# Row block 0 in two mapped halves, and early columns for both layers right behind rows 0 and 1

## The chip, the cores and the metric

The kernel runs on one core of a Trainium2 chip, as one program. The metric is device time in microseconds (us) of one execution. All data is float32.

## The reference

The network is two graph layers over N = 8192 nodes with F = 64 features and one dense 8192 x 8192 matrix `adj`:

```
x_drop  = x * (u >= 0.1) / 0.9
x1      = layernorm(x + adj @ x_drop)              # first layer
proj    = tanh(|x1|) * x1 / (|x1| + 1e-8)          # |.| is the row's norm, clipped to 10
support = adj @ proj                               # second layer: adj a second time
out     = arctanh(min(|s|, 0.999)) * s / (|s| + 1e-8) @ kernel + bias     # s: rows of support
result  = layernorm(x1 + out)
```

`adj` is 256 MB, far more than the chip's on-chip memory. The second layer needs `proj`, and row block r of `proj` needs all of row block r of `adj @ x_drop`.

## The kernel before

`adj` is cut into 16 x 16 blocks of 512 x 512 elements (1 MB each), block (r, c) for row block r and column block c. A block is loaded by one DMA from the SP queue into a slot of `ring` (17 slots; at the end two more in `feats`). TensorE multiplies it, transposed, in 4 tiles of 128 contraction rows: `feats[:, 0]` (the dropped x, 64 wide) or `feats[:, 1]` (the projection) is the weight, the block's 512 columns are the moving operand, and sums go to a PSUM bank as 64 x 512. Two matmuls of one step go to the two halves of a bank (partitions 0 to 63 and 64 to 127). One layer of one block is 4 matmuls, both layers are 8. The trace shows each matmul as two records, so a layer of a block is 8 records.

`work_order` writes all steps in one list, and every engine follows it:

- `first`: a block used for layer 1 alone, into `sums_first`, 4 matmuls; it is loaded again later. `hold`: the same, but it stays in the ring until its column is mapped.
- `both`: block (r, c) with c < r, both layers, 8 matmuls into `sums_both`: the column is already mapped when row r comes.
- `early`: block (r, 0) for r = 2 to 15, both layers, right behind the start of row 1, in runs of 5 (`EARLY_RUN`). Bank: `sums_both[0]` for even rows, `sums_part[3]` for odd rows. ScalarE saves the layer 2 half in `support` (L416); VectorE turns the layer 1 half in 8 transposes and adds it to x (`early_end`, L501 to 505).
- `part`: layer 2 alone, for held blocks of a column just mapped or for blocks loaded again, one row or two rows in a bank (`two_halves`, `two_rows`); VectorE adds the bank to `support`.
- `turn`: row block r is complete in layer 1. ScalarE copies one half of the sums (L422), VectorE joins, turns, normalises and maps it (`layer1_join`, `layer1_end`), with a power on GpSimd (L374) and the tanh on ScalarE (L427) between. The semaphore `mapped` then lets TensorE use column r for layer 2.
- `finish`: the final part for one or two rows: the product with the weight matrix, arctanh, the residual and the last layernorm.

Behind each turn the next row's lead (`lead_of`, 7 units of 4 matmuls) needs nothing from it, so that TensorE has work while the turn runs. `HELD` says how many blocks of a row are held, `REREAD` how many blocks are loaded again ahead of a row. `place_blocks` gives each load its slot and the number of releases (`block_released`) that SP waits for.

Row block 0 is 12 `first` and 4 `hold` steps; the 8 chunks of x and u (`xu`, 512 KB each) are loaded between its blocks, one chunk per two column blocks. There are 335 block loads in all.

## Time and profile before

| | |
|---|---|
| median of 3 runs | 938.77 us (938.63 to 939.33) |
| the profiled execution, its own time | 938.78 us |
| span of the profile | 936.5 us |
| between the two | 2.28 us |
| TensorE busy | 898.3 us (96%) |
| DMA | 358.35 MB, 383 GB/s over the span |
| VectorE, ScalarE, GpSimd busy | 287.1, 52.0, 57.4 us |

The span runs from the first to the last instruction. A busy TensorE is one with a matmul record open. The kernel's time outside the span is the same small piece at the launch. The rows themselves stand in a section further down.

### The profile page before, as it was taken

How to read it: one execution, taken by the hardware profiler on the slowest of the kernel's cores; microseconds unless marked ns; L12 is line 12 of the kernel's file. 1: busy time of each engine (PE TensorE's matmuls, PEld its weight loads, DVE VectorE, ACT ScalarE, POOL GpSimd, SP SyncE). 2: the span in 40 equal slices, each digit the busy share in tenths (PEclk: the TensorE clock that was granted, in tenths of full speed). 3: DMA queues.
4: the chain of work that ended last, by engine and by line, in shares of the span. 5: the costliest groups of instructions: out<-in, count | busy, mean ns of one | idle time of the engine just before them, and what ended most of it. 6: DMA issues, size and time to landing. Idle time of an engine off the chain costs nothing.

```text
span 936.5 us, 10555 instructions
## 1 busy us (share of the span) xinstructions
PE 898.3 (96%) x4224; PEld 300.9 (32%) x4224; DVE 287.1 (31%) x1056; ACT 52.0 (6%) x136; POOL 57.4 (6%) x50
## 2 busy tenths in 40 slices
PE   5669999999999999999999999999999999999995
PEld 1113333333333333333333333333333333333332
DVE  1135464322313040403131140402204021056656
ACT  0001010000000000000000000000000000002332
POOL 0000000000000000000000000000000000002322
PEclk9999999999999999999999999999999999999998
DMA  9999999999999999997979989799998999999994
GB/s 378 418 422 421 421 421 416 421 422 420 421 421 421 421 413 421 347 423 270 408 289 400 384 333 375 271 424 385 356 356 304 423 362 354 317 399 421 420 421 182
DMA packets 52319, 358.35 MB, mean 383 GB/s; under 512 B 6320, under 2 KB 8368, under 8 KB 9392
## 3 DMA queue, kind: packets, MB, share of 16 engines
q1 hardware_dynamic: 51696, 357.55, 94.6%
q8 instruction: 34, 0.56, 0.2%
q10 hardware_dynamic: 576, 0.13, 0.1%
q14 instruction: 13, 0.11, 0.0%
HBM read 355.57 MB, written 2.10 MB: 382 GB/s over the span
## 4 chain that ended last, share of the span: by engine, by line
PE 88%; DMA 8%; SPq 2%; DVE 1%; issue 0%; POOL 0%; ACT 0%; DVEq 0%
PE sums_both L698 39%; PE sums_first L652 20%; PE sums_part L661 20%; DMA ring<-adj_dram 8%; PE sums_part L652 4%; PE sums_part L680 3%; PE sums_both L680 3%; SPq L339 1%; PE sums_first L742 0%; PE sums_both L742 0%; SPq L335 0%; DVE rows_in L604 0%; DVE stats L478 0%; DVE mv L481 0%; PE sums_both L737 0%
## 5 line engine op out<-in xcount | busy, mean ns | idle before, releaser
L698 PE MATMUL sums_both<-ring,feats 128*64 128x512 f32 x1696 | 370.1, 592 | 0.5 <-DMA ring<-adj_dram 0.5
L652 PE MATMUL sums_first<-ring,feats 128*64 128x512 f32 x1088 | 247.1, 600 | 26.7 <-DMA ring<-adj_dram 26.7
L698 PEld LDWEIGHTS sums_both<-ring,feats 128*64 128x64 f32 x1696 | 121.7, 137 | 243.0 <-issue 240.9
L661 PE MATMUL sums_part<-ring,feats 128*64 128x512 f32 x816 | 182.9, 593 | 0.0
L652 PEld LDWEIGHTS sums_first<-ring,feats 128*64 128x64 f32 x1088 | 76.7, 138 | 190.6 <-issue 142.1
L488 DVE TENSOR_TENSOR row_saved<-sums_both,row_saved 64x512 f32<-64x512 f32 x15 | 10.2, 682 | 350.9 <-ACT row_saved L422 350.9
L661 PEld LDWEIGHTS sums_part<-ring,feats 128*64 128x64 f32 x816 | 59.2, 137 | 114.2 <-issue 113.6
L374 POOL TENSOR_TENSOR rooted<-base,power 128x8 f32<-128x8 f32 x16 | 27.8, 1737 | 799.8 <-DVE base L514 799.8
L553 DVE TENSOR_TENSOR rows_in<-sums_part,rows_in 128x512 f32<-128x512 f32 x36 | 24.9, 692 | 133.8 <-PE sums_part L661 133.6
L652 PE MATMUL sums_part<-ring,feats 128*64 128x512 f32 x240 | 54.7, 593 | 0.0
L422 ACT COPY row_saved<-sums_first 64x512 f32<-64x512 f32 x16 | 9.3, 580 | 606.0 <-PE sums_first L652 606.0
L498 DVE STREAM_TRANSPOSE turned<-row_saved 32x128 f32<-32x128 f32 x128 | 38.6, 302 | 2.1
L652 PEld LDWEIGHTS sums_part<-ring,feats 128*64 128x64 f32 x240 | 17.0, 137 | 32.9 <-issue 32.0
L680 PE MATMUL sums_both<-ring,feats 128*64 128x512 f32 x112 | 25.2, 592 | 0.0
L680 PE MATMUL sums_part<-ring,feats 128*64 128x512 f32 x112 | 25.2, 592 | 0.0
L498 DVE STREAM_TRANSPOSE turned<-sums_part 32x128 f32<-32x128 f32 x56 | 17.2, 308 | 14.0 <-PE sums_part L680 13.2
L406 ACT ACTIVATE rows_in<-rows_in,shift,rooted 128x64 f32<-128x64 f32 x60 | 20.7, 427 | 6.9 <-POOL shift L367 6.8
L498 DVE STREAM_TRANSPOSE turned<-sums_both 32x128 f32<-32x128 f32 x56 | 17.2, 308 | 10.2 <-PE sums_both L680 9.5
L559 DVE TENSOR_TENSOR rows_in<-sums_part,rows_in 64x512 f32<-64x512 f32 x16 | 10.9, 682 | 27.0 <-PE sums_part L652 26.9
L383 POOL TENSOR_TENSOR rooted<-base,power 128x8 f32<-128x8 f32 (+1 forms) x9 | 13.5, 1496 | 48.5 <-DVE base L570 48.5
L472 DVE TENSOR_SCALAR rows_in<-rows_in 128x512 f32<-128x512 f32 x8 | 3.4, 427 | 40.4 <-DMA rows_in<-xu_dram 40.4
L364 POOL TENSOR_TENSOR rooted<-base,power 128x8 f32<-128x8 f32 (+1 forms) x9 | 13.5, 1496 | 22.3 <-DVE minus_mean L613 19.3
(72 smaller groups left out, 246.6 us busy)
## 6 DMA issues: line engine op xcount, KB each, us to landing
ring<-adj_dram SPq DMA_DIRECT2D x331, 1024.0 KB, 12.7
rows_in<-xu_dram SPq DMA_DIRECT2D x8, 512.0 KB, 20.1
feats<-adj_dram SPq DMA_DIRECT2D x4, 1024.0 KB, 16.2
out_dram<-rows_in SPq DMA_DIRECT2D x15, 128.0 KB, 6.9
out_dram<-rows_in SPq DMA_DIRECT2D x1, 96.0 KB, 2.0
selw<-selector_dram ACTq DMA_DIRECT2D x1, 32.0 KB, 6.6
selw<-weight_dram ACTq DMA_DIRECT2D x1, 32.0 KB, 10.1
bias_sb<-bias_dram ACTq DMA_DIRECT2D x1, 32.0 KB, 12.3
```

The source lines that it names most:

```text
L364: nc.gpsimd.tensor_tensor(rooted[:, 0, own], base[:, 0, own], power[:, 0, own], ALU.pow).then_inc(deviation_ready, 1)
L374: nc.gpsimd.tensor_tensor(rooted[:, :, 0:TB], base[:, :, 0:TB], power[:, :, 0:TB], ALU.pow).then_inc(root_ready, 1)
L383: nc.gpsimd.tensor_tensor(rooted[:, 1, own], base[:, 1, own], power[:, 1, own], ALU.pow).then_inc(norm_rooted, 1)
L406: last = nc.scalar.activation(x_row(r)[:, t, :], x_row(r)[:, t, :], ACT.Identity, scale=rooted[:, 0, i:i + 1], bias=shift[:, i:i + 1])
L488: done(V.tensor_tensor(row_sum[:], sums_both[r % 2][0:F], half_sum[:], ALU.add))
L498: last = V.transpose(turned[q:q + Q, :, f:f + Q], tiles[f:f + Q, :, q:q + Q])
L553: V.tensor_tensor(total, bank[:], total, ALU.add).then_inc(part_added, 1)
L559: done(V.tensor_tensor(total, bank[0:F], total, ALU.add))
L652: last = nc.tensor.matmul(bank[at:at + F], feats[:, which, c * TB + t, :], block_of(slot)[:, t, :], start=start and t < 2, stop=stop and t ...
L661: last = nc.tensor.matmul(bank[F * g:F * g + F], feats[:, 1, c * TB + t, :], block_of(slot)[:, t, :], start=start and t == 0, stop=stop an ...
L680: last = nc.tensor.matmul(early_banks[r % 2][layer * F:layer * F + F], feats[:, layer, t, :], block_of(slot)[:, t, :], start=t == 0, stop= ...
L698: last = nc.tensor.matmul(sums_both[r % 2][layer * F:layer * F + F], feats[:, layer, c * TB + t, :], block_of(slot)[:, t, :], start=begin ...
```

## The change

Row block 0 is loaded in another cut: a 1 MB pack holds two column blocks for 256 of the 512 rows. The kernel runs over all columns for the first 256 rows (8 `top` steps, h = 0), then for the second (h = 1), with matmuls of 256 moving columns; each half has a `turn` of its own, with 2 tiles in place of 4. Directly behind come `begin` and `complete` for (r, 0), r = 2 to 7: `begin` uses tiles 0 and 1 (the first mapped half of column 0) in both layers, `complete` tiles 2 and 3, each 4 matmuls, into six banks. For rows 2 to 5 the block is loaded in two halves of 512 KB (`lower`, `upper`). The lead of row 1 is empty. `early` of column 0 for rows 8 to 12 follows, and behind row 1's turn `early` for (13, 0), (14, 0), (15, 0), later columns 1 of rows 13 to 15, and `again` for column 1 of rows 7 to 12 (both layers, into `sums_part[2]` and `[3]`, added by VectorE). The saved early sums stay unturned: ScalarE copies them in two pieces of 64 x 256 to the row's own place in `feats[:, 1]`, and `early_join` adds them at the end of the row. When row 0 is loaded again, a `strip` load puts one column block together from two runs of 4 KB a partition; a held block of row 0 is read by the matmul from two slots, as 2 x 256 columns. `HELD[11]` is 4 in place of 3. There are 334 MB of block loads.

TensorE's instructions between row 0 and the first `part` of column 1. In `before` (a name is written tile<-operands, the last figure is the count of matmuls):

```order
L652 MATMUL sums_first<-ring,feats 64x512 x92
L652 MATMUL sums_part<-ring,feats 64x512 x4
L680 MATMUL sums_both<-ring,feats 64x512 x8
L680 MATMUL sums_part<-ring,feats 64x512 x8
L680 MATMUL sums_both<-ring,feats 64x512 x8
L680 MATMUL sums_part<-ring,feats 64x512 x8
L680 MATMUL sums_both<-ring,feats 64x512 x8
L652 MATMUL sums_first<-ring,feats 64x512 x16
L698 MATMUL sums_both<-ring,feats 64x512 x8
```

The same place in the changed kernel:

```order
L838 MATMUL sums_first<-ring,feats 64x256 x128
L856 MATMUL sums_both<-ring,feats 64x512 x8
L856 MATMUL sums_part<-ring,feats 64x512 x16
L856 MATMUL sums_both<-ring,feats 64x512 x8
L856 MATMUL sums_part<-ring,feats 64x512 x16
L810 MATMUL sums_part<-ring,feats 64x512 x4
L856 MATMUL sums_both<-ring,feats 64x512 x8
L856 MATMUL sums_part<-ring,feats 64x512 x8
L856 MATMUL sums_both<-ring,feats 64x512 x8
L856 MATMUL sums_part<-ring,feats 64x512 x8
L856 MATMUL sums_both<-ring,feats 64x512 x8
L810 MATMUL sums_first<-ring,feats 64x512 x44
```

The 92 matmuls of layer 1 were row 0 (64) and seven blocks of row 1 (28). Now row 0 stands alone as 128 matmuls of half the width, and 48 matmuls of column 0 for both layers come directly behind it; row 1's blocks come after.

TensorE behind row 1's last block, in the changed kernel (`L869` is `again`, `L819` a part of two rows):

```order
L810 MATMUL sums_first<-ring,feats 64x512 x16
L856 MATMUL sums_part<-ring,feats 64x512 x16
L856 MATMUL sums_both<-ring,feats 64x512 x8
L810 MATMUL sums_first<-ring,feats 64x512 x4
L819 MATMUL sums_part<-ring,feats 64x512 x8
L856 MATMUL sums_part<-ring,feats 64x512 x16
L856 MATMUL sums_both<-ring,feats 64x512 x8
L869 MATMUL sums_part<-ring,feats 64x512 x16
L810 MATMUL sums_first<-ring,feats 64x512 x8
L869 MATMUL sums_part<-ring,feats 64x512 x16
```

Before, the 28 matmuls between row 1's last block and the part of column 1 were seven layer 1 blocks of row 2; now they are the three early blocks and one such block, again 28.

VectorE for one early block, before:

```order
L557 COPY rows_in<-sums_part 64x512
L560 TENSOR_TENSOR rows_in<-sums_part,rows_in 64x512
L498 STREAM_TRANSPOSE turned<-sums_both 32x4x32 x8
L505 TENSOR_TENSOR rows_in<-turned,rows_in 128x256
L498 STREAM_TRANSPOSE turned<-sums_part 32x4x32 x8
L505 TENSOR_TENSOR rows_in<-turned,rows_in 128x256
```

and where these transposes stood, behind the first part and up to row 1's join, now:

```order
L708 COPY rows_in<-sums_part 64x512
L711 TENSOR_TENSOR rows_in<-sums_part,rows_in 64x512
L641 TENSOR_TENSOR row_saved<-sums_both,row_saved 64x512
L642 TENSOR_TENSOR row_saved<-sums_first,row_saved 64x512
L654 STREAM_TRANSPOSE turned<-row_saved 32x4x32 x8
L662 TENSOR_TENSOR y<-turned,rows_in 128x256
```

All 14 pairs of transposes and addition are gone from VectorE's list ahead of row 1's join.

The core of the diff:

```diff
+FIRST_OF_TWO = 13
+AGAIN = (7, 8, 9, 10, 11, 12)
+AGAIN_RUN = 2
+BEGUN = (2, 3, 4, 5, 6, 7)
+SPLIT = (2, 3, 4, 5)
...
         if r == 0:
-            order += firsts + holds + [("turn", 0)]
+            for h in range(2):
+                order += [("top", 0, pair, h) for pair in range(NB // 2 - 1, -1, -1)] + [("turn", 0, h)]
+            order += [("begin", row, 0) for row in BEGUN] + [("complete", row, 0) for row in BEGUN]
             continue
-        lead, rest = lead_of([("both", r, c) for c in range(r >= 2, r - 1)] + firsts)
+        ahead = [("early", row, 0) for row in range(FIRST_OF_TWO, NB)] if r == 2 else []
+        lead, rest = ([], firsts) if r == 1 else lead_of(ahead + [("both", r, c) for c in range(columns_early(r), r - 1)] + firsts)
...
+        if r == 2:
+            order += [("early", row, 1) for row in range(FIRST_OF_TWO, NB)]
+            rest += holds[:-1]
+            again = [("again", row, 1) for row in AGAIN]
+            while again:
+                order += again[:AGAIN_RUN] + rest[:AGAIN_RUN]
+                again, rest = again[AGAIN_RUN:], rest[AGAIN_RUN:]
...
+                if kind == "strip":
+                    own = slice(c % 2 * HALF_TILES, (c % 2 + 1) * HALF_TILES)
+                    sp.dma_start(block_of(slot).rearrange("p (h t) w -> p h (t w)", h=2),
+                                 adj[0, c - c % 2:c - c % 2 + 2, :, own, :].rearrange("h p t w -> p h (t w)")
+                                 ).then_inc(block_loaded[slot], 16)
...
                     act.wait_ge(block_released, uses[i][1])
-                    nc.scalar.copy(support[half(r), r // 2], early_banks[r % 2][F:P]).then_inc(early_saved, 1)
+                    nc.scalar.copy(early_sums(r)[0:F], early_bank(r)[0:F, 0:HALF])
+                    nc.scalar.copy(early_sums(r)[F:P], early_bank(r)[0:F, HALF:BS])
+                    nc.scalar.copy(support[half(r), r // 2], early_bank(r)[F:P]).then_inc(early_saved, 1)
...
+                if kind == "top":
+                    h = step[3]
+                    pe.wait_ge(dropped, 1 + chunk_order.index(c))
+                    for col in (2 * c, 2 * c + 1):
+                        for t in range(TB):
+                            at = F * (t % 2)
+                            last = nc.tensor.matmul(sums_first[h][at:at + F, 0:HALF], feats[:, 0, col * TB + t, :],
+                                                    pack_of(slot)[:, col % 2, t, :],
+                                                    start=col == NB - 2 and t < 2, stop=col == 1 and t >= TB - 2)
...
+                    if kind == "complete" and r in SPLIT:
+                        pe.wait_ge(rest_loaded[r], 16)
+                    pe.wait_ge(mapped, turn_of(c, kind != "begin"))
+                    for t in range(HALF_TILES if kind == "complete" else 0, HALF_TILES if kind == "begin" else TB):
...
+                if kind == "again":
+                    k = AGAIN.index(r)
+                    pe.wait_ge(early_saved, bank_saved(again_banks[k % 2]))
+                    if k >= 2:
+                        pe.wait_ge(again_added, k - 1)
+                    pe.wait_ge(mapped, turn_of(c))
```

## Rows read from the trace of the kernel before

**Rows 1.** The page: span, and TensorE's share.

```profile
span 936.5 us, 10555 instructions
PE 898.3 (96%) x4224; PEld 300.9 (32%) x4224; DVE 287.1 (31%) x1056; ACT 52.0 (6%) x136; POOL 57.4 (6%) x50
```

**Rows 2.** Stretches: us, busy (records) of each engine, clock, DMA share, GB/s.

```profile
core 0: us, PE busy (x) PEld busy (x) DVE busy (x) ACT busy (x) POOL busy (x), PEclk, DMA share, GB/s
7.20:55.40 48.20, 33.53 (x128) 8.58 (x128) 7.84 (x14) 0.00 (x0) 0.00 (x0) 1.00 1.01 420
55.40:73.80 18.40, 13.59 (x58) 3.68 (x60) 6.86 (x28) 0.79 (x2) 1.67 (x1) 1.00 1.02 423
73.80:206.90 133.10, 132.56 (x616) 43.98 (x612) 61.45 (x194) 10.66 (x20) 3.49 (x2) 1.00 1.01 420
300.00:900.00 600.00, 600.00 (x2860) 203.69 (x2858) 155.71 (x574) 24.82 (x70) 35.12 (x25) 1.00 0.94 372
```

**Rows 3.** TensorE's waits: for whom, us, times, longest.

```profile
PE sums_first L652 <- DMA ring<-adj_dram: 26.7, 21, 7.2
...
PE sums_both L698 <- DMA ring<-adj_dram: 0.5, 1, 0.5
```

**Rows 4.** TensorE in order of time: start, us, what, idle before.

```profile
47.18 1.94 PE L652 MATMUL sums_first<-ring,feats 128*64 128x512 f32 x8 [0.55 <-DMA ring<-adj_dram]
50.94 1.94 PE L652 MATMUL sums_first<-ring,feats 128*64 128x512 f32 x8 [1.83 <-DMA ring<-adj_dram]
53.43 1.94 PE L652 MATMUL sums_first<-ring,feats 128*64 128x512 f32 x8 [0.55 <-DMA ring<-adj_dram]
56.90 1.94 PE L652 MATMUL sums_first<-ring,feats 128*64 128x512 f32 x8 [1.54 <-DMA ring<-adj_dram]
...
71.83 1.94 PE L652 MATMUL sums_first<-ring,feats 128*64 128x512 f32 x8 [0.54 <-DMA ring<-adj_dram]
73.60 1.89 PE L652 MATMUL sums_part<-ring,feats 128*64 128x512 f32 x8
```

**Rows 5.** TensorE in order of time, around the one later wait.

```profile
206.94 5.37 PE L698 MATMUL sums_both<-ring,feats 128*64 128x512 f32 x24 [0.55 <-DMA ring<-adj_dram]
```

**Rows 6.** The chain of waits, in order of time: start, us, what.

```profile
139.00 13.73 PE sums_first L652 x64
152.73 3.43 PE sums_part L661 x16
...
730.74 27.46 PE sums_both L698 x128
...
902.99 1.09 PE sums_both L742 x16
```

**Rows 7.** Row 0's turn, ScalarE's first and VectorE's last row of it.

```profile
55.41 0.58 ACT L422 COPY row_saved<-sums_first 64x512 f32<-64x512 f32 x1 [53.40 <-PE sums_first L652]
...
64.58 0.42 DVE L531 TENSOR_TENSOR feats<-rows_in,scale 128x256 f32<-128x256 f32 x1
```

**Rows 8.** VectorE around row 1's turn.

```profile
141.71 0.42 DVE L505 TENSOR_TENSOR rows_in<-turned,rows_in 128x256 f32<-128x256 f32 x1
142.17 0.68 DVE L488 TENSOR_TENSOR row_saved<-sums_both,row_saved 64x512 f32<-64x512 f32 x1
...
151.44 0.42 DVE L531 TENSOR_TENSOR feats<-rows_in,scale 128x256 f32<-128x256 f32 x1
```

**Rows 9.** Groups of ScalarE and VectorE by form: count, busy, mean ns of one.

```profile
L416 ACT COPY rows_in<-sums_both 64x512 f32<-64x512 f32 x7 | 4.1, 582 | 37.5 <-PE sums_both L680 37.5
L444 ACT ACTIVATE row_saved<-sums_both 128x256 f32<-128x256 f32 x8 | 2.6, 371 | 16.0 <-PE sums_both L742 16.0
L488 DVE TENSOR_TENSOR row_saved<-sums_both,row_saved 64x512 f32<-64x512 f32 x15 | 10.2, 682 | 350.9 <-ACT row_saved L422 350.9
```

**Rows 10.** The page's DMA issues: count, KB each, us to landing.

```profile
rows_in<-xu_dram SPq DMA_DIRECT2D x8, 512.0 KB, 20.1
```

More of the change, by code:

```diff
@@ L107, in lead_of @@
         while n < len(blocks) and work < LEAD:
-            work += 2 if blocks[n][0] == "both" else 1
+            work += 1 if blocks[n][0] == "first" else 2
             n += 1
@@ L122, in work_order @@
             rest += holds[:-1]
-            early = [("early", row, 0) for row in range(2, NB)]
+            early = [("early", row, 0) for row in range(BEGUN[-1] + 1, FIRST_OF_TWO)]
             while early:
@@ L224, in ended_at, with last_early, turn_of @@
         return ([k - 1] if 0 < k < len(groups) - 1 else []) + ([k] if k >= len(groups) - 2 else [])
+    def last_early(r):
+        return 0 if r < FIRST_OF_TWO else 1
     def saved_through(r):
-        return min(1 + 2 * r, 2 + r)
+        return r + 3
+    def turn_of(r, h=1):
+        return r + h + 1
+    saved_at = {row: k + 1 for k, row in enumerate(
+        s[1] for s in order if s[0] == "complete" or s[0] == "early" and s[2] == last_early(s[1]))}
+    unsignalled = [i for i, (_, _, count) in uses.items() if order[i][0] == "part" and not count]
     with ExitStack() as es:
```

304 lines of the change are left out of this document (209 added, 95 removed).

## The prediction

> **What bounds the kernel now.** I read the page first: TensorE is busy 898.3 of 936.5 us [rows 1], so the end is close to its work, and the question is where the other 38 us are. The list of waits names 26.7 us behind the block loads at L652 and only 0.5 us behind them elsewhere [rows 3]. The table by stretches says when: up to 73.8 us TensorE is partly idle while the DMA runs at 420 GB/s; from 73.8 to 900 it is practically never idle [rows 2]. The order of time gives the last start with a regular wait, 71.83 us [rows 4], and the single later one, 0.55 us at 206.94 [rows 5]. The granted clock is 1.00 in all of these stretches, the 2.4 GHz level, although TensorE is busy only 33.53 of 48.20 us in the first of them [rows 2]. So from 71.83 us to the last projection the kernel lasts as long as its matmuls, and what the start leaves undone is paid in full later.
>
> Two paces carry everything. TensorE: 128 records of both-layer work take 27.46 us [rows 6]; a matmul is two records, so it takes 0.4291 us, one layer of a block (4 matmuls) 1.72 us, both layers 3.43 us. Loads: six blocks from 56.90 to 71.83 are 2.49 us each [rows 4]. The wait at 206.94 is for block 76 (counted from 0 in order of use: rows 0 and 1 with 16 each, 14 early blocks, rows 2 and 3 with 15 each come before it), that at 71.83 for block 22, hence (206.94 - 71.83)/54 = 2.50 us a block. A layer 1 block therefore leaves TensorE idle 0.78 us per load, a block for both layers gains 0.93 us on the loads.
>
> **The change part by part.**
>
> *Row 0's loads.* The same 16 MB of blocks and 4 MB of x and u go through the same queue, so the last of the 16 packs can start when block 15 did: 53.43 us [rows 4]. Its 8 matmuls of half the width are 1.72 us if 256 columns cost half of 512. TensorE is free at 55.15.
>
> *What is left at that point.* Before, when block 22 starts at 71.83, 22 x 4 = 88 matmuls of 2048 are done and TensorE then never stops, so 1960 follow. Now, at 53.43, 15 packs are done, worth 60, and 1988 follow. If TensorE does not stop from there on, the end comes earlier by (71.83 - 53.43) - 28 x 0.4291 = 18.40 - 12.01 = 6.39 us. That is the main term: row 1's seven layer 1 blocks, which were run with 0.78 us idle each, now come when there is a backlog.
>
> *Is there work without a stop?* After 55.15 come six `begin` steps and six `complete` steps of 1.72 us. Loads behind the last pack: four halves (1.25 us each), two whole blocks, four halves. Between block 15 and block 16 the trace has 3.47 us in place of 2.49 [rows 4], 0.98 more, cause not visible; I take both cases. Without it the loads are in at 54.7, 55.9, 57.2, 58.4, 60.9, 63.4, the steps want them at 55.2, 56.9, 58.6, 60.3, 62.0, 63.7: no stop. With it the first comes at 55.7 (0.5 late) and (7, 0) at 64.4 (0.1 late): 0.6 us. The second halves are in at 64.7 to 68.4 (or 1 us later) and wanted from 65.5. Value 0.30 us, ends 0 and 0.6. `begin` needs the first half mapped: the first 12 MB are in by 53.43 - 8 x 2.49 = 33.5, and a full-size turn lasts from 55.41 to 65.00 [rows 7], 9.6 us, so this one is over by 45. `complete` needs the second half: from 55.4 with at most those 9.6 us to 65.0, wanted at 65.5. Row 0's turn with half the tiles should be nearer to 8 us; the cover is 0.5 us even at full length.
>
> *The next tight load* is block (13, 0), the 28th MB behind the last pack: in at 53.43 + 6 x 2.49 + 22 x 2.50 = 123.4 (124.4 with the 0.98). TensorE gets there after 160 matmuls: 55.15 + 68.7 = 123.8, and 124.4 with the 0.6 us already lost. Nothing is added in either case.
>
> *The wait of 0.55 us* [rows 5] goes. By block (4, 1) nine more blocks have been used for both layers (three of column 1 for rows 13 to 15, six `again`; the rest are only moved). It is due at 206.9 + 9 x 2.50 = 229.4; TensorE would be there at 206.4 - 6.4 + 9 x 3.43 = 230.9. Cover 1.5 us. Past 300 us the DMA share is 0.94 while TensorE is busy 600.00 of 600.00 [rows 2], so the loads are ahead, and the order of the steps there stays. Credit 0.55 us, ends 0 and 0.55.
>
> *Row 1's turn.* Today its join starts at 142.17, right behind the transposes of row 15's early sums (to 142.13), and the last write is at 151.86 [rows 8]; TensorE uses it at 152.73 [rows 6], 0.87 us later. The transposes are gone, so VectorE is free when row 1 ends, and the lead is again 28 matmuls (12.0 us). The cover grows; (15, 0), which waits for the bank that row 1 used, has two early blocks (6.9 us) ahead of it against two copies of 0.58 and two additions of 0.68 [rows 9]. From row 2 on the join begins beside ScalarE's copy. Value 0.
>
> *Saving the early sums.* Three ScalarE copies a row: one of 64 x 512 is 0.58 us; one of 64 x 256 isn't in the trace, above 0.37 (128 x 256, L444) at the lowest and 0.58 at the highest [rows 9]. That is 1.3 to 1.75 us a row against 1.72 us for a `complete` and 3.43 for an `early`. The first bank wanted again soon is row 7's, for row 9, after 1.72 + 3.43 = 5.15 us: free in time from either end. `again` adds three VectorE instructions, at most 3 x 0.69 = 2.1 us, and a bank rests at least two both-layer steps. Value 0, ends 0 and 1 us for the hand-offs together.
>
> *Row 0's second use.* 64 matmuls (16 columns) now read 2 x 256 columns from two places. Every moving operand in the trace is one run. Value 0, as both runs are 1 KB long; from the other side it is a rival below. The half-size loads: x and u are such loads (512 KB [rows 10]), and 1 MB of block with 0.5 MB of them takes 50.94 - 47.18 = 3.76 us [rows 4], 2.50 per MB, the pace of whole blocks. Value 0. Against it stands a rule of the Trainium skill ("DMA: Bandwidth & Descriptors", section Bandwidth): batch DMAs to at least 1 MiB to get 75% of peak or more. By that rule the eight halves behind row 0 would be slow; this trace does not agree, since its 512 KB loads run at 420 GB/s in the stretch to 55.40 [rows 2], queued behind each other. By the rows the sum is as above; the rule would make it the third rival's.
>
> *The end.* Two more parts in all, a few steps exchanged, but the last five groups and their chain stay; the loads become 334 from 335 MB where nobody waits for them. Value 0.
>
> Sum: 6.39 + 0.55 - 0.30 = 6.6 us. The profiled execution is 938.78 us, of which 2.28 lie outside the span, and the median is 938.77; the forecast is 932.2 us. Own range: 6.9 (no late load) and a little for the turn at the top, 5.3 (0.6 us late, 1 us of hand-offs, the 0.55 kept) below: 931.7 to 933.5.
>
> **The rivals.**
>
> *Weight loads set the pace of the packs.* They are not halved. 612 of them are busy 43.98 us [rows 2], 0.072 us each, and a record of 256 columns is 0.107. If they don't hide, a pack of 16 records takes 2.86 us against a load of 2.49. The second half's packs start at 36.0, the eighth ends at 58.9 and not 55.15: 3.7 us, less the 0.3 of late loads. 935.6 us. For: half the matmul time to hide in. Against: at full width nothing of them shows, and 16 records of 128 columns take 1.09 us [rows 6], 0.068 each, less than 0.072 and the matmul's 0.053 in line. 8%.
>
> *A hand-off is short.* The mapped second half (0.5 us of cover), a bank not saved or an addition queued behind a turn: 1 to 4 us, so about 935. For: six banks and three kinds of step are new. Against: the covers above. 6%.
>
> *The half-size loads are slow.* At three quarters of the pace the eight halves (4 MB) cost 3.3 us more, all of it in front of steps with 0.5 us of cover: 935.3 us. Against: the pair of 3.76 us. 2%.
>
> *The loads are the limit and give nothing back.* If behind the start the pace were 2.62 us a block, block (4, 1) would be as late as the gain is big, and the time stays near 938.8. Against: 2.50 measured over 54 blocks and 1.5 us of cover. 3%.
>
> *Slower: the moving operand in two runs.* If each of the 64 matmuls of row 0's second layer loses time at the break, all of it lands on a TensorE that is never idle. It decides from 6.6/64 = 0.10 us each, a quarter of a matmul; at twice the time it is 27 us and 959 us. For: no row shows such an operand, and the held ones lie in two slots. Against: nothing but the length of the runs. 4%.
>
> **How the numbers follow.** The forecast has 77%. The first three rivals are still faster. A measurement of this kernel tells 0.2% (1.9 us) from no change. Faster: 77 + 8 + 6 + 2 less one for a hand-off at its dearest, 92%; same: 4% (the loads, and that one); slower: 4%. The range takes the forecast's own and reaches to the first rivals: 931.4 to 935.8, with about 12% left out.
>
> **What the profile would show.** TensorE without a wait from 53.4 us on, its last L838 group near there and `begin` close to 55.2; the waits for loads of ring at some 24 us; a pack of 16 records in 1.9 us; the first layer-2 part (row 0 alone) near 76 us; no wait at the block of row 4 and column 1, near 231 us; the parts with row 0 at 0.43 us a matmul. I am wrong if packs take 2.8 us, if a TensorE wait for ScalarE or VectorE of over 1 us stands between 55 and 200 us, or if row 0's parts take longer than other rows'.

## The result and the profile after

The median went from 938.89 us (938.63 to 939.43) to 933.75 us (932.53 to 936.03, six runs), a ratio of 0.9946 [0.9936, 0.9957]. The forecast was 932.2 us in a range of 931.4 to 935.8. So the gain is 5.1 of the 6.6 us that the sum had. The six runs of the changed kernel lie 3.5 us apart, those of the kernel before 0.8 us, and the execution that was profiled is the slowest of the six, 936.03 us. What it shows of waits is therefore likely more than the median run has. With the repeats further down the changed kernel has 18 runs, from 932.53 to 937.07 us with a median of 934.09, and the kernel before 68 runs, from 938.44 to 940.98 us with a median of 938.91: the gain over all of them is 4.8 us.

The page of the changed kernel: span, and the engines' shares (beside [rows 1]).

```profile
span 934.1 us, 10819 instructions
PE 897.3 (96%) x4352; PEld 332.2 (36%) x4352; DVE 273.7 (29%) x1000; ACT 62.6 (7%) x166; POOL 57.8 (6%) x51
```

There are 128 more matmul records: row 0's 64 matmuls of the first layer are now 128 of half the width. VectorE has 13 us less work, ScalarE 11 us more. Both have room. Outside the span lie 936.03 - 934.1 = 1.93 us, and not the 2.28 of the kernel before; behind the last projection the span is longer by the same 0.35 us, so the comparison below goes by the last projection.

TensorE's waits in the changed kernel (for whom, us, times, longest), beside [rows 3]:

```profile
PE sums_first L838 <- DMA ring<-adj_dram: 22.7, 15, 7.0
PE sums_part L819 <- issue: 1.3, 2, 1.1
PE sums_first L810 <- DMA ring<-adj_dram: 0.8, 2, 0.6
PE sums_both L927 <- DVE rows_in L701: 0.6, 1, 0.6
PE sums_part L856 <- DMA ring<-adj_dram: 0.5, 1, 0.5
```

The 26.7 us of [rows 3] have become 22.7, as the row 1 blocks no longer wait. But three rows (L819, L810, L856) are stops that the sum did not have. TensorE in order of time says where (start, us, what, idle before), beside [rows 4] and [rows 5]:

```profile
29.55 1.95 PE L838 MATMUL sums_first<-ring,feats 128*64 128x256 f32 x16 [1.82 <-DMA ring<-adj_dram]
34.54 1.95 PE L838 MATMUL sums_first<-ring,feats 128*64 128x256 f32 x16 [3.04 <-DMA ring<-adj_dram]
...
54.42 1.95 PE L838 MATMUL sums_first<-ring,feats 128*64 128x256 f32 x16 [0.54 <-DMA ring<-adj_dram]
56.20 3.60 PE L856 MATMUL sums_both<-ring,feats 128*64 128x512 f32 x16
...
76.86 1.89 PE L810 MATMUL sums_part<-ring,feats 128*64 128x512 f32 x8
...
121.88 1.94 PE L810 MATMUL sums_first<-ring,feats 128*64 128x512 f32 x8 [0.22 <-DMA ring<-adj_dram]
124.38 1.94 PE L810 MATMUL sums_first<-ring,feats 128*64 128x512 f32 x8 [0.56 <-DMA ring<-adj_dram]
126.86 7.09 PE L856 MATMUL sums_part<-ring,feats 128*64 128x512 f32 x32 [0.55 <-DMA ring<-adj_dram]
...
521.25 3.65 PE L819 MATMUL sums_part<-ring,feats 128*64 128x512 f32 x16 [1.06 <-issue]
624.76 3.65 PE L819 MATMUL sums_part<-ring,feats 128*64 128x512 f32 x16 [0.28 <-issue]
922.23 1.16 PE L927 MATMUL sums_both<-selw,rows_in 128*128 128x128 f32 x8 [0.63 <-DVE rows_in L701]
```

A pack lasts as a whole block did (1.95 us for 16 records), the first `begin` starts at 56.20 right behind the last pack, the first layer 2 part at 76.86, and nothing waits at block (4, 1) near 233 us. The last pack starts at 54.42, not at 53.43. Before it is one gap of 4.99 us (29.55 to 34.54) where [rows 4] have 3.76 for a block with x and u. Then come three stops at 121.88, 124.38 and 126.86, at the last two blocks of row 1, (1, 2) and (1, 1), and at (13, 0); and two at 521 and 625 us, where the steps behind them read blocks of rows 2 and 3 again. The view calls the last two "issue", so that they are waits for loads is inferred from their place and not shown.

The chain of waits (start, us, what), beside [rows 6]:

```profile
139.10 3.43 PE sums_part L819 x16
...
233.51 6.87 PE sums_both L886 x32
...
786.34 30.90 PE sums_both L886 x144
...
922.23 1.17 PE sums_both L927 x8
```

L819 at 139.10 is row 0's second layer: an operand in two runs takes the usual 3.43 us for 16 records. The 144 records at 786.34 take 30.90 us, 0.2146 each, as in [rows 6]. So TensorE works at the pace it had.

**Where the time is.** From 56.20 to the last projection at 922.23 are 866.03 us. Before it was 73.60 to 925.00 [rows 4], 851.40, with 28 matmuls less to do (12.01 us). How much a stop costs is in [rows 4]: blocks start every 2.49 us and need 1.72, so 0.77 us are idle, of which the view names 0.55. Each stop costs 0.22 us beside its wait (the group in front of a stop is shown with 1.94 us and not 1.72). So the kernel before worked 851.40 - 0.77 = 850.63 us, the one after should take 862.64, and 866.03 means 3.39 us of stops. The five waits add up to 2.67, with 0.22 each to 3.77: the account closes within 0.4 us. In seven more profiles of the changed kernel and its variants it closes within 0.55 us.

| | forecast | profiled execution |
|---|---|---|
| start of the backlog less 28 matmuls | 6.39 | 17.40 - 12.01 = 5.39 |
| the stop at 206.94 that goes | 0.55 | 0.77 |
| late loads behind row 0 | -0.30 | 0 |
| stops that are new (the remainder; the waits alone give -3.77) | 0 | -3.39 |
| sum | 6.64 | 2.77 (938.78 - 936.03 = 2.75) |

### The profile page after: what moved, and what is told of

It reads as the page before. It is cut to its first block, busy times and chain, and to the rows that moved or that the text cites. A ratio compares the mean times of both kernels' runs of the same rounds, so it can differ in the third digit from the quotient of the medians.

```text
span 934.1 us, 10819 instructions
## 1 busy us (share of the span) xinstructions
PE 897.3 (96%) x4352; PEld 332.2 (36%) x4352; DVE 273.7 (29%) x1000; ACT 62.6 (7%) x166; POOL 57.8 (6%) x51
## 4 chain that ended last, share of the span: by engine, by line
PE 89%; DMA 6%; SPq 3%; DVE 1%; issue 0%; POOL 0%; ACT 0%; DVEq 0%
PE sums_both L886 35%; PE sums_first L810 20%; PE sums_part L819 19%; DMA ring<-adj_dram 6%; PE sums_part L810 5%; PE sums_part L856 4%; PE sums_both L856 3%; PE sums_part L869 2%; SPq L444 2%; SPq L439 1%; PE sums_first L932 0%; PE sums_both L932 0%; DVE rows_in L755 0%; DVE stats L603 0%; PE sums_first L838 0%
## 5 line engine op out<-in xcount | busy, mean ns | idle before, releaser
L886 PE MATMUL sums_both<-ring,feats 128*64 128x512 f32 x1552 | 339.4, 592 | 0.0
L810 PE MATMUL sums_first<-ring,feats 128*64 128x512 f32 x960 | 212.7, 592 | 0.8 <-DMA ring<-adj_dram 0.8
L886 PEld LDWEIGHTS sums_both<-ring,feats 128*64 128x64 f32 x1552 | 125.2, 137 | 207.8 <-issue 206.7
L819 PE MATMUL sums_part<-ring,feats 128*64 128x512 f32 x800 | 180.3, 593 | 1.3 <-issue 1.3
L810 PEld LDWEIGHTS sums_first<-ring,feats 128*64 128x64 f32 x960 | 71.2, 137 | 136.0 <-issue 133.1
L819 PEld LDWEIGHTS sums_part<-ring,feats 128*64 128x64 f32 x800 | 61.9, 137 | 109.8 <-issue 109.2
L634 DVE TENSOR_TENSOR row_saved<-sums_both,feats 64x256 f32<-64x256 f32 x28 | 11.7, 416 | 228.5 <-PE sums_both L886 228.3
L810 PE MATMUL sums_part<-ring,feats 128*64 128x512 f32 x256 | 58.7, 593 | 0.0
L838 PE MATMUL sums_first<-ring,feats 128*64 128x256 f32 x256 | 33.6, 408 | 22.7 <-DMA ring<-adj_dram 22.7
L654 DVE STREAM_TRANSPOSE turned<-row_saved 32x128 f32<-32x128 f32 (+1 forms) x136 | 40.0, 294 | 2.2
L856 PE MATMUL sums_part<-ring,feats 128*64 128x512 f32 x160 | 35.5, 593 | 0.5 <-DMA ring<-adj_dram 0.5
L810 PEld LDWEIGHTS sums_part<-ring,feats 128*64 128x64 f32 x256 | 19.6, 137 | 34.2 <-issue 34.0
L838 PEld LDWEIGHTS sums_first<-ring,feats 128*64 128x64 f32 x256 | 18.0, 145 | 38.0 <-DMA ring<-adj_dram 29.9
L645 DVE TENSOR_TENSOR row_saved<-sums_first,row_saved 64x512 f32<-64x512 f32 x14 | 9.6, 682 | 73.6 <-PE sums_first L810 73.6
L856 PE MATMUL sums_both<-ring,feats 128*64 128x512 f32 x112 | 25.2, 592 | 0.0
L869 PE MATMUL sums_part<-ring,feats 128*64 128x512 f32 x96 | 21.1, 592 | 0.0
L856 PEld LDWEIGHTS sums_part<-ring,feats 128*64 128x64 f32 x160 | 11.3, 137 | 23.8 <-issue 21.7
```

Of the source, the lines that this page charges most:

```text
L654: last = V.transpose(turned[q:q + Q, 0:n, f:f + Q], tiles[f:f + Q, 0:n, q:q + Q])
L810: last = nc.tensor.matmul(sums_for(row, bank[at:at + F]), feats[:, which, c * TB + t, :], moving(row, c, t, own), start=start and t < 2, s ...
L819: last = nc.tensor.matmul(sums_for(r[g], bank[F * g:F * g + F]), feats[:, 1, c * TB + t, :], moving(r[g], c, t, own), start=start and t == ...
L838: last = nc.tensor.matmul(sums_first[h][at:at + F, 0:HALF], feats[:, 0, col * TB + t, :], pack_of(slot)[:, col % 2, t, :], start=col == NB ...
L856: last = nc.tensor.matmul(early_bank(r)[layer * F:layer * F + F], feats[:, layer, c * TB + t, :], block_of(slot)[:, t, :], start=c + t == ...
L869: last = nc.tensor.matmul(again_banks[k % 2][layer * F:layer * F + F], feats[:, layer, c * TB + t, :], block_of(slot)[:, t, :], start=t == ...
```

## Experiments

Ratios are against the kernel before, run beside them on the same chip; medians of the kernel before in those calls lie between 938.76 and 939.09 us.

**The changed kernel again, twice (no edit).**

> The changed kernel itself, once more. Its profiled execution was the slowest of six (936.03 against a median of 933.75) and lost 1.3 us in waits for loads from 121.9 to 126.9 us and 1.3 us at 521 and 625 us. Theory A (a load lands late when code loading has taken one DMA engine for a while, so the cover of 0 to 1 us at these places is used up in some executions and not in others): the median stays 933 to 934.5 us, executions spread over 2 us or more, and in the new profile these waits have other sizes, with TensorE's last pack of row 0 again near 54.4 us. Rival B (the waits are built into the order): the same waits to 0.1 us, and a spread as small as that of the kernel before (0.8 us).

> The changed kernel again, beside the two before on one chip: 933.5 to 936 us, ratio to before 0.994 to 0.997, waits for loads of 0.3 to 2.7 us in all behind 55 us, at the same three places (65.5, 121 to 127, 520 to 625 us) but of other sizes.

Measured: 935.8 us (932.93 to 937.07), ratio 0.9958 [0.9944, 0.9971], and 933.67 us (932.88 to 936.83), ratio 0.995 [0.9937, 0.9962]. The first median is above the 934.5 us that were expected, and 5 of the 18 runs lie above 935.8. TensorE of the first, behind row 0:

```profile
65.52 1.94 PE L856 MATMUL sums_part<-ring,feats 128*64 128x512 f32 x8 [0.35 <-DMA ring<-adj_dram]
...
126.05 7.09 PE L856 MATMUL sums_part<-ring,feats 128*64 128x512 f32 x32 [0.23 <-DMA ring<-adj_dram]
520.43 3.65 PE L819 MATMUL sums_part<-ring,feats 128*64 128x512 f32 x16 [1.04 <-issue]
559.17 3.65 PE L886 MATMUL sums_both<-ring,feats 128*64 128x512 f32 x16 [0.75 <-DMA ring<-adj_dram]
```

The second has 0.31, 0.54 and 0.55 us from 123.10 to 128.06, 0.39 at 521.79, 0.55 at 550.03, and a stop of 0.76 at 69.35 that was not expected, at the step for the second half of (3, 0) ("issue" in the view): 3.10 us in all, more than the 2.7 expected. The places mostly come back (the gap near 34 us in both, 65 to 69, 122 to 128, 520, 550 to 560), the sizes do not. By the medians the gain is 5.1, 3.2 and 5.1 us in the three measurements. How late the loads are differs from execution to execution.

**No half-size loads (the first four blocks of column 0 behind row 0 are loaded whole; row 0 itself keeps its two halves and two turns).**

```diff
-SPLIT = (2, 3, 4, 5)
+SPLIT = ()
```

> SPLIT is empty: the first four blocks behind row 0 are loaded whole and not in halves. Theory A: the six begin steps then wait for whole blocks at 2.49 us each; (7, 0) can start at 54.4 + 6 x 2.49 = 69.4 us and not at 64.8, 4.6 us later; 1.3 us of that come back at block (13, 0), where the changed kernel waited for its load: 937.1 us, between 936.5 and 938.5. Rival: the halves are only a detail (TensorE has backlog enough later on): 933.8 us.

Measured: 938.0 us (936.98 to 939.51), ratio 0.9987 [0.9978, 0.9995]. TensorE:

```profile
54.34 1.95 PE L838 MATMUL sums_first<-ring,feats 128*64 128x256 f32 x16 [0.53 <-DMA ring<-adj_dram]
56.82 1.94 PE L856 MATMUL sums_both<-ring,feats 128*64 128x512 f32 x8 [0.54 <-DMA ring<-adj_dram]
...
69.25 1.94 PE L856 MATMUL sums_part<-ring,feats 128*64 128x512 f32 x8 [0.54 <-DMA ring<-adj_dram]
```

Six one-layer steps wait for a load each, 6 x 0.77 = 4.6 us idle. The median is 2.2 us above the changed kernel's in the same call (935.8) and 3.9 above that of its 18 runs. So the half-size loads are most of the gain, as they give TensorE two steps of 1.72 us for each 2 x 1.25 us of loads. Nothing waits near 124 us here; three stops stand at 549 to 562 us (0.37, 0.55 and 0.61).

The experiment shows a price of the half-size loads too, which the prediction had put at nothing. With whole loads (7, 0) follows the last pack by 69.25 - 54.34 = 14.91 us, 2.485 for each of six blocks. With halves there are 4 MB between the two, 9.94 us at that pace; the profile with the 65.52 above has 65.52 - 54.63 = 10.89, 0.95 us late, and two more have 0.95 and 1.06. The table by stretches agrees. This kernel, the changed kernel, and the one with halves up to row 7 (further down), in this order:

```profile
54.00:72.00 18.00, 14.39 (x70) 4.52 (x72) 5.13 (x24) 0.57 (x2) 1.01 (x1) 1.00 1.01 421
54.00:72.00 18.00, 17.58 (x90) 6.43 (x92) 5.13 (x24) 3.27 (x9) 1.02 (x1) 1.00 1.01 411
54.00:72.00 18.00, 17.46 (x92) 6.50 (x92) 5.13 (x24) 3.19 (x8) 1.02 (x1) 1.00 1.01 377
```

The last figure is GB/s, at the same DMA share. The kernel before has 421 there too. All seven profiles with eight halves have 401 to 411, both with twelve 377 and 376. That is 0.4 to 0.9 us of loads lost by the eight and 1.9 by the twelve. Whether it is their size, their 4 KB runs or that four of them follow each other, no run separates: the x and u chunks are 512 KB as well and cost nothing between whole blocks (3.76 us for 1.5 MB in [rows 4]).

**No column 1 early.**

```diff
-FIRST_OF_TWO = 13
-AGAIN = (7, 8, 9, 10, 11, 12)
+FIRST_OF_TWO = NB
+AGAIN = ()
...
-                    if start and n in (2, 3):
+                    if start and n in (2, 3) and AGAIN:
```

> Column 1 is not used early for any row (AGAIN empty, rows 13 to 15 take column 0 early like the others); row 0 in two halves and the steps behind it stay. Theory A (the loads up to block (4, 1) set the time, whatever TensorE does before): TensorE waits some 7 us for loads between 125 and 210 us, block (4, 1) starts near 207 us as in the kernel before, and the whole gain is gone: 938.5 us, between 937.8 and 939.5. Rival B (the gain is made in the first 75 us and stays): 933.8 us.

Measured: 941.61 us (941.41 to 942.33), ratio 1.0029 [1.0018, 1.004]: slower than the kernel before, and 2 us above the top of what was expected. TensorE:

```profile
54.31 1.95 PE L838 MATMUL sums_first<-ring,feats 128*64 128x256 f32 x16 [0.55 <-DMA ring<-adj_dram]
57.12 3.65 PE L856 MATMUL sums_both<-ring,feats 128*64 128x512 f32 x16 [0.86 <-DMA ring<-adj_dram]
144.19 1.94 PE L810 MATMUL sums_first<-ring,feats 128*64 128x512 f32 x8 [0.55 <-DMA ring<-adj_dram]
...
209.24 7.09 PE L886 MATMUL sums_both<-ring,feats 128*64 128x512 f32 x32 [0.54 <-DMA ring<-adj_dram]
```

TensorE runs into the loads nine times between 144 and 185 us and once more at (4, 1), which starts 2.30 us later than in [rows 5]. Up to (4, 1) the loads set the time here, as they did before; what the start wins is given back, and what makes the loads later is paid in full. They are 0.88 us later at the last pack (54.31 against 53.43). From there 61 blocks take 209.24 - 54.31 = 154.93 us, against 152.04 in the kernel with 40 small matmuls below, which also has its gap in front and loads nothing in halves: 2.89 us more, and the stretch from 54 to 72 us ran at 403 GB/s. Without column 1 the new start is worth less than nothing; column 1 early with whole loads, the experiment before this, has 0.13%; both together have 0.5%.

**The kernel before with a shorter lead.**

```diff
-        lead, rest = lead_of([("both", r, c) for c in range(r >= 2, r - 1)] + firsts)
+        lead, rest = (firsts[:4], firsts[4:]) if r == 1 else lead_of([("both", r, c) for c in range(r >= 2, r - 1)] + firsts)
```

> The kernel before, with the lead of row 1 cut from seven layer 1 blocks to four, so that the early blocks start three loads sooner; nothing else. At the start alone it gains 3 x 0.78 = 2.3 us of TensorE time. Theory A: all of it is given back as waits for loads before block (4, 1), which starts at 206.9 us again: 938.9 us (938.3 to 939.4). Rival B: 936.6 us.

Measured: 938.87 us (938.67 to 940.41), ratio 1.0002 [0.9994, 1.0011]. TensorE:

```profile
64.47 1.94 PE L652 MATMUL sums_first<-ring,feats 128*64 128x512 f32 x8 [0.55 <-DMA ring<-adj_dram]
169.59 3.65 PE L698 MATMUL sums_both<-ring,feats 128*64 128x512 f32 x16 [0.18 <-DMA ring<-adj_dram]
177.04 1.94 PE L652 MATMUL sums_first<-ring,feats 128*64 128x512 f32 x8 [0.36 <-DMA ring<-adj_dram]
...
206.84 7.09 PE L698 MATMUL sums_both<-ring,feats 128*64 128x512 f32 x32 [0.56 <-DMA ring<-adj_dram]
```

Three waits at the start go (the last is at 64.47, not 71.83), four come at 169 to 182, and (4, 1) starts where it did. This is the same lesson from the other side: a better start alone wins nothing here.

**Where does the 0.98 us come from? The kernel before with 40 small matmuls at its start**, which do nothing but make TensorE's program longer.

```diff
+            V.memset(blank[:], 0.0).then_inc(blank_set, 1)
...
+            pe.wait_ge(blank_set, 1)
+            for _ in range(40):
+                nc.tensor.matmul(sums_both[0][0:F, 0:F], blank[:, 0:F], blank[:, F:2 * F], start=True, stop=True)
```

> The kernel before with 40 small matmuls (64 columns) of a blank tile at its very start, while TensorE has nothing loaded yet: 160 more records and nothing else. Theory A (loads land 1 us late each time code is loaded, since that takes one of the DMA engines; TensorE's code is loaded every few hundred instructions): the gap of 3.47 us between the starts of blocks 15 and 16 goes (2.49 there), and the same 1 us appears about nine blocks sooner, between blocks 5 and 8 (starts 22 to 29 us), because TensorE gets there with 160 instructions more behind it. Time within 1.2 us of the kernel before. Rival B (the gap belongs to the place, to a transfer or to row 0's turn): it stays between blocks 15 and 16.

Measured: 939.25 us (938.55 to 941.05), ratio 1.0005 [0.9996, 1.0014]. TensorE:

```profile
9.50 1.94 PE L658 MATMUL sums_first<-ring,feats 128*64 128x512 f32 x8 [0.18 <-DMA ring<-adj_dram]
14.69 5.35 PE L658 MATMUL sums_first<-ring,feats 128*64 128x512 f32 x16 [3.25 <-DMA ring<-adj_dram]
...
54.66 1.94 PE L658 MATMUL sums_first<-ring,feats 128*64 128x512 f32 x8 [0.54 <-DMA ring<-adj_dram]
57.14 1.94 PE L658 MATMUL sums_first<-ring,feats 128*64 128x512 f32 x8 [0.54 <-DMA ring<-adj_dram]
```

The gap of 3.47 us between blocks 15 and 16 [rows 4] is 2.48 now, and block 15 itself is 1.23 us later than at 53.43: the lateness has moved ahead, to block 2 (sooner than the blocks 5 to 8 that were expected). In the DMA view the queue named "instruction" has one packet of 16 KB at just these places (queue, kind: packets, MB, share of 16 engines). The kernel before, 53 to 58 us, around its gap; then the changed kernel, 30 to 36 us, around its gap of 4.99 us; then the kernel with 40 small matmuls, 10 to 16 us, around its gap:

```profile
q8 instruction: 1, 0.02, 1.3%
...
q8 instruction: 1, 0.02, 1.1%
...
q8 instruction: 1, 0.02, 1.1%
```

A share of 1.3% of 16 engines in 5 us is 1.04 us of one engine. In steps of 5 us up to 55 us, these are the first such packets of each kernel (50 to 55 in the one before holds its only one). TensorE had started a similar number of records by the three gaps, 240, 224 and 192, half of them matmuls and half weight loads, though the times are 53, 34 and 15 us (one line of the table by stretches for each, in the same order):

```profile
0.00:53.40 53.40, 31.59 (x120) 8.10 (x120) 8.96 (x16) 1.28 (x1) 0.34 (x6) 1.00 0.98 401
0.00:34.50 34.50, 16.10 (x112) 8.43 (x112) 8.96 (x16) 1.28 (x1) 0.34 (x6) 1.00 0.96 391
0.00:14.60 14.60, 10.21 (x96) 7.42 (x96) 2.40 (x5) 1.28 (x1) 0.34 (x6) 1.00 0.89 353
```

So the gap goes with how far TensorE is in its code and not with the block or the time, and rival B is out. Over all profiles it is 0.8 to 1.5 us. The later packets, every 20 to 45 us, mostly add no gap where blocks still arrive one by one: this kernel has its second one between 55 and 60 us, and its blocks stay 2.47 us apart. One does: without column 1 early, the packet between 50 and 55 us took 4.0% and not 1.3 to 1.4%, and TensorE waits 0.86 us at 57.12, where the changed kernel goes on at 56.20. One reading fits most of it: a packet of code holds up one of the 16 DMA engines for 1 us; a load has landed when its slowest engine is done; with a queue that is always full that engine stays behind, and a later packet on another engine usually makes nothing later. The Trainium skill ("DMA: Bandwidth & Descriptors", section Why a DMA increments its semaphore by 16 and not by 1) says that a DMA runs on up to 16 engines that finish independently and that the semaphore counts them; the trace agrees with that as far as the size goes, 0.8 to 1.5 us of lateness against 1.0 to 1.1 us of one engine, but doesn't show the single engines. Shown is that the gap moves with the code; the mechanism is argued.

**Row 0's second loads whole (one run for each moving operand).** The input holds a second copy of row 0 for it.

```diff
-                    sp.dma_start(block_of(slot).rearrange("p (h t) w -> p h (t w)", h=2),
-                                 adj[0, c - c % 2:c - c % 2 + 2, :, own, :].rearrange("h p t w -> p h (t w)")
-                                 ).then_inc(block_loaded[slot], 16)
+                    sp.dma_start(block_of(slot), whole[c]).then_inc(block_loaded[slot], 16)
```

> The changed kernel with row 0's second loads in the plain cut (a second copy of row 0 in the input): whole blocks with 8 KB a partition in place of two runs of 4 KB, and a moving operand in one run; only the held blocks still lie in two slots. Theory A (neither the two runs nor the 4 KB cost anything): as the changed kernel, 933 to 936.5 us, waits for loads at 121 to 127 us and 0 to 1.5 us between 500 and 630 us remain. Rival B (the strip loads are late and cause the wait of 1.0 us at 520): no wait there, 1 us faster.

Measured: 934.24 us (932.83 to 934.99), ratio 0.9947 [0.9934, 0.9959], the changed kernel's time; the changed kernel itself was not run in this call. Its profiled execution is one of the fastest here (span 931.0, 932.83 us), and this is the only wait for a load behind its last pack:

```profile
125.25 7.09 PE L853 MATMUL sums_part<-ring,feats 128*64 128x512 f32 x32 [0.28 <-DMA ring<-adj_dram]
919.13 1.16 PE L924 MATMUL sums_both<-selw,rows_in 128*128 128x128 f32 x8 [0.64 <-DVE rows_in L698]
```

This is what an execution with hardly any stop looks like: 5.87 us ahead of the kernel before at the last projection. A moving operand in one run gains nothing that the time shows. About the loads in two runs the result is divided: the time is as theory A has it, but the wait at 520 us is missing, as rival B has it. It stands in the three profiles of the changed kernel and in the one with halves up to row 7 (1.06, 1.04, 0.39, 0.44 us), not in this one, though TensorE gets there earliest here. That the loads in two runs make it likelier is not excluded; one profile can't tell.

**Fewer held slots, to free loads in the middle.**

```diff
-HELD = [4, 4, 4, 3, 5, 4, 3, 5, 6, 5, 4, 4, 3, 2, 1, 1]
+HELD = [4, 4, 4, 3, 5, 3, 3, 5, 5, 5, 4, 4, 3, 2, 1, 1]
```

> The changed kernel with HELD[5] 3 for 4 and HELD[8] 5 for 6: two slots more are free when rows 9 to 12 are at work, so loads are issued sooner; two blocks more are loaded again. Theory A (the waits at 520, 559 and 625 us come from too few free slots, so that a load that lands late is felt at once): TensorE waits for no load after 130 us, 1.0 to 1.8 us faster than the changed kernel, ratio to before near 0.994. Rival B (the two loads more cost as much): no gain.

Measured: 934.88 us (933.39 to 935.65), ratio 0.9951 [0.9938, 0.9963]. No wait is left between 130 and 900 us, but there is a new one at the end:

```profile
126.99 7.09 PE L856 MATMUL sums_part<-ring,feats 128*64 128x512 f32 x32 [0.54 <-DMA ring<-adj_dram]
918.57 1.94 PE L810 MATMUL sums_part<-feats 128*64 128x512 f32 x8 [0.34 <-DMA feats<-adj_dram]
```

Two waits for loads stand in front as well, 0.46 us at 65.50 and 0.43 at 124.51. That fits held slots as a cause of the stops in the middle (the two other profiles with `HELD[8]` 5, below, have none there either), but the profile before this one has none either, with the slots as they were. That the blocks loaded again make the end late is not shown: the kernel before with its early sums unturned, further down, reads nothing more and waits 0.20 and 0.56 us there, too. The time is the same as the changed kernel's, and the gain of 1.0 to 1.8 us that was expected is not there.

**The same, and one row more of column 1 early**, for the stops at (13, 0).

```diff
-EARLY_RUN = 5
-FIRST_OF_TWO = 13
-AGAIN = (7, 8, 9, 10, 11, 12)
+EARLY_RUN = 6
+FIRST_OF_TWO = 14
+AGAIN = (7, 8, 9, 10, 11, 12, 13)
```

> As the one before, and row 13 is treated like rows 7 to 12: (13, 0) comes with the early blocks of rows 8 to 12, its column 1 as an again step (FIRST_OF_TWO 14, EARLY_RUN 6). The load that TensorE waited for near 122 to 127 us then has 0.9 us more cover. Expected: 0.2 to 1.3 us faster than the one before, ratio to before near 0.993, 932.2 us; nothing left of the waits between 100 and 700 us but at most 0.4 us.

Measured: 933.82 us (933.39 to 935.02), ratio 0.9949 [0.9935, 0.9963]. It is 1.1 us faster than the one before, as expected, but not at the 932.2 us that were. Its profile (933.39 us) has 0.35 us at 65.41 and 0.32 at 917.15, no other. The stops in the middle and at (13, 0) are gone, and the median is no better than the changed kernel's 933.75 and 933.67; only its spread is smaller, 1.6 us in five runs.

**The early sums alone kept unturned, in the kernel before**: two ScalarE copies in place of VectorE's transposes of each.

```diff
+                    nc.scalar.copy(early_sums(r)[0:F], early_banks[r % 2][0:F, 0:BS // 2])
+                    nc.scalar.copy(early_sums(r)[F:P], early_banks[r % 2][0:F, BS // 2:BS])
...
-                turn(early_banks[r % 2][0:F].rearrange("p (t n) -> p t n", n=P)).then_inc(early_turned, 1)
-                dve.wait_ge(early_turned, r - 1)
-                done(V.tensor_tensor(x_row(r), turned[:], x_row(r), ALU.add))
```

> The kernel before with its early sums kept unturned (two ScalarE copies of 64 x 256 a row into feats, added by VectorE at the end of the row) and nothing else of the change. Theory: no change (938.5 to 939.5 us, ratio 1.000), since TensorE waits neither for VectorE nor for ScalarE before or after; row 1's join starts at once behind its copies (0.7 us sooner than the 142.17 us of before). Rival (the shorter work ahead of row 1's turn is part of the gain): 0.5 us or more faster.

Measured: 939.07 us (938.61 to 940.03), ratio 1.0002 [0.9993, 1.0011]. Row 1's join starts at 141.68 and not at 142.17 [rows 8], 0.49 us sooner (0.7 was expected), and TensorE doesn't notice. The profiled execution, 939.92 us, has two waits for loads at the end (0.20 and 0.56 us at 921.09 and 923.59) that account for the 1.1 us above 938.78: the kernel before, too, has slower executions from late loads. This part of the change costs and brings nothing by itself; it is what lets six sums be kept at once.

**Halves up to row 7.**

```diff
-SPLIT = (2, 3, 4, 5)
+SPLIT = (2, 3, 4, 5, 6, 7)
```

> The changed kernel with all six blocks behind row 0 loaded in halves (SPLIT 2 to 7). The wait of 0.35 to 0.46 us at (7, 0), 65.5 us, seen in three of five profiles, goes (1.25 us more cover for (6, 0) and 2.5 for (7, 0)); where it was not, the time is the same. Expected: 0 to 0.6 us faster than the control of this call.

Measured: 936.41 us (935.07 to 938.02), ratio 0.9973 [0.9964, 0.9982]: 2.7 us slower than the changed kernel in the same call (933.67; 2.1 by the means) and not a little faster. The wait at 65.5 is gone, the ones behind are larger:

```profile
122.43 1.94 PE L810 MATMUL sums_first<-ring,feats 128*64 128x512 f32 x8 [0.38 <-DMA ring<-adj_dram]
...
127.41 7.09 PE L856 MATMUL sums_part<-ring,feats 128*64 128x512 f32 x32 [0.55 <-DMA ring<-adj_dram]
521.18 3.65 PE L819 MATMUL sums_part<-ring,feats 128*64 128x512 f32 x16 [0.44 <-issue]
```

The early wait was only put off: a stop that is saved at 65 us is one at 124. Twelve half-size loads in place of eight take more from the loads, 377 GB/s from 54 to 72 us in place of 401 to 411 (above), 1.9 us of loads in place of 0.4 to 0.9. That is a likely cause of the loss, but not shown to be all of it: the one profile is of a faster execution (935.58 us), and its stops add up to 2.8 us, no more than in the changed kernel.

**Three of these ideas together** (halves up to row 7, row 13 early in both columns, `HELD[8]` 5).

> The changed kernel with SPLIT 2 to 7, row 13 among the again rows (FIRST_OF_TWO 14, EARLY_RUN 6) and HELD[8] 5 for 6 (HELD[5] stays 4, so one load more and not two). All places where a profile showed TensorE waiting for a load behind 55 us get 0.9 to 2.5 us more cover. Expected: 1.0 to 2.0 us faster than the control, ratio to before near 0.993, and a profile without a wait for loads between 56 us and the last projection.

Measured: 934.91 us (933.87 to 935.59), ratio 0.9955 [0.9943, 0.9967]. No gain (1.2 us above the changed kernel in the same call, where 1 to 2 less were expected): 0.17, 0.55 and 0.55 us at 125.30 to 130.26 and 0.36 at 233.84, now also at (4, 1). No version was faster than the changed kernel by more than the intervals.

## Why the prediction was right, and where it was off

*The mechanism held.* The end came forward because TensorE is hardly idle behind the last pack, so what counts is how early that state begins. Four of the five rivals did not happen: packs take 1.95 us, not 2.86 (the weight loads hide), the operand in two runs is at 3.43 us for 16 records and costs nothing, the loads behind the start are not at 2.62 us a block (the 70 up to (4, 1) take at most (233.51 - 54.42)/70 = 2.56 each), and no wait for ScalarE or VectorE stands between 55 and 200 us. (The 0.072 us of the first rival is no duration: it is busy time divided by a count of loads that overlap. The pages of the two kernels have 137 ns for one load, and 145 for one of a pack.) Half a turn took VectorE from 56.88 to 63.93 us; with the copy at 56.41 that is 7.5 us, near the 8 of the forecast. ScalarE's three copies a row are 0.37, 0.36 and 0.58 us, 1.31 together, at the lower end of the bounds.

*The fifth rival, slow half-size loads, happened in part.* The prediction gave them the pace of whole blocks ("Value 0"), from x and u chunks that lie between whole blocks. Eight in a row cost 0.4 to 0.9 us by the bytes moved, and (7, 0), behind four of them, came up to 1.06 us late in three profiles. The times of the rival, 3.3 us and 935.3, did not come, as most of the loss fell where TensorE had cover.

*The main term, 6.39 us, measured 5.39.* It took 53.43 us for the last pack from the kernel before, where the 0.98 us gap came one block later. Now the gap comes before: the last pack starts at 54.42, and in the other profiles of the changed kernel at 54.63 and 54.50. The prediction saw the gap, wrote "cause not visible" and put it behind the last pack, with a value of 0.30 us. It belongs to the code and not to the block: the changed kernel's packs have twice the instructions, so the gap comes at 34 us already, and it had to be charged to the start.

*"Nothing is added in either case" at (13, 0) failed.* The two sides were 123.8 and 123.4 there, or both 124.4: a cover of 0 to 0.4 us. Three stops stand there, 1.33 us of waits and 0.66 us of restarts. TensorE wanted the block at 56.20 + 68.65 = 124.85; the load was not in at the 124.4 of the late case but at 126.86, 72.44 us behind the last pack and not 69.9. Over the profiles with eight halves that stop there these 28 MB take 71.1 to 73.6 us, 1.2 to 3.7 more than at the pace of whole blocks. The halves' lower rate accounts for 0.4 to 0.9 of it; the rest is open. A cover of that size should have had a price in the sum, as the 0.5 us at 65.5 should have, where three of the later profiles have 0.35 to 0.46 us.

*"The loads are ahead, and the order of the steps there stays" past 300 us failed.* The share of 0.94 in [rows 2] was an average. 1.34 us of waits at 521 and 625 us, and others at 550 to 560 in the two repeats, show that an average hides places without cover. With fewer held slots they were gone, but with row 0 loaded whole they were gone, too, so few free slots are a likely cause and not a shown one. The kernel before has 0 us there. That TensorE was later in it is not enough to explain this: with whole loads behind row 0 the last projection is as late as before (925.11), and three stops stand at 549 to 562 us.

*The credit at 206.94 was too small.* A stop costs 0.77 us and not the 0.55 that the view names. The prediction had used 0.78 for the same stops two paragraphs before.

*What nets out.* Terms that were too good by 1.0 and 3.4 us, against 0.2 and 0.3 too bad, make 3.9 us in the execution that was profiled, which at 936.03 us lies outside the range. The median is 1.55 us above the forecast, and the one clean execution, 932.83 us, is within 0.7 us of it.

*What was luck.* The lower end of the gain was added up wrong: 6.39 less 0.6 for late loads and 1.0 for hand-offs, with the 0.55 kept, is 4.8 and not 5.3, so the forecast's own range should have ended at 934.0 and not at 933.5. The median of 933.75 is past the end as written and inside the right one. It is there partly because 1.0 us was set aside for hand-offs, which cost nothing, while stops that the sum did not have cost more. The wider range, to 935.8, was drawn for rivals; one repeat has its median just there, and 5 of the 18 runs lie beyond. So the mechanism and the size of the main term are understood, and that the number fell within the range owes something to allowances made for other reasons.

Why one execution is later than another stays open. Over all runs the spread is 2.5 us before (68 runs) and 4.5 us after (18 runs). That it grew because TensorE now runs within about a microsecond of its loads in five places is argued, not shown.

## What to carry to other kernels

When two resources are close to each other for the whole run, a gain at the start is a loan: before counting it, find every later place where the saved time would bring the fast engine up to its loads (here (13, 0), 520, 560 us), and pay for it there. Where the change also cuts the transfers in another way, take their pace from a row in which they follow each other as they will, not from one where they lie between large ones. The two parts of such a change can each be worth next to nothing or less, and 5 us together, so a part that shows no gain by itself is not yet refuted. And a cover of a few tenths of a microsecond is no cover: as a rule of thumb, give it half the price of a stop, restart included.

## What the runs showed of the hardware

- The first 16 KB packet of the queue named "instruction" (34 packets in 0.56 MB) comes with a gap of 0.8 to 1.5 us, after which the loads of a full queue stay late by it; 40 more matmuls at the start moved the gap from 56.9 to 14.7 us. Longer code on the engine that is watched can so cost time without being slower itself. That the packet is the cause is argued.
- A stop of TensorE for a load costs 0.22 us more than the wait that the profile names: starts 2.49 us apart with 1.72 us of work and 0.55 us of wait.
- Half-size loads (512 KB, in 4 KB runs) that follow each other in a full queue run below the pace of 1 MB loads: from 54 to 72 us 421 GB/s without them, 401 to 411 with eight, 376 and 377 with twelve. The rule of the Trainium skill ("DMA: Bandwidth & Descriptors", section Bandwidth), to batch DMAs to 1 MiB for 75% of peak or more, has the direction right here; the loss is 2 to 5% of the rate with eight and 11% with twelve. An average over a long stretch hides it: from 55 to 127 us the changed kernel moved 420 GB/s.
